# A two-layer bias-and-mix kernel: TensorE tiles of 64x64 and 64x32, and ten regions in place of nine

## What is computed

```python
# layer 0: x[h, q, k] += bias[q, k, h]
rel = tril(q - k)
nd = log(|c * rel| + 1) / (log(|c * max(rel.max(-1), threshold)| + 1) + 1e-6)
bias = relu(nd[..., None] * W1 + b1) @ W2 + b2
# layer 1, on x of shape (M=16, T=1024, S=1024)
ret = einsum('MTS,MN->NTS', x, w + eye)
ret += einsum('ITS,TIM->MTS', einsum('MTS,TIM->ITS', x, qw1), qw2)   # rank 2, per row t
ret += einsum('ITS,SIM->MTS', einsum('MTS,SIM->ITS', x, kw1), kw2)   # rank 2, per column s
ret += x * qdd[t, m] + x * kdd[s, m]                                 # diagonals
```

## Time and profile before

| | us |
|---|---|
| median of 3 runs | 911.21 |
| lowest and highest run | 910.2, 916.39 |
| span of the profiled execution | 930.2 |

### The profile page before, as it was taken

The page is one execution under the profiler, slowest core; times in us unless marked ns, Lnnn a source line. Parts: engine busy times, 40 slices in busy tenths (PEclk is TensorE's granted clock), DMA queues, the critical chain, the costliest instruction groups (busy, mean ns, idle before and its releaser), DMA issues. The chain is left out here.

```text
span 930.2 us, 39085 instructions
## 1 busy us (share of the span) xinstructions
PE 741.4 (80%) x18210; PEld 547.7 (59%) x18210; DVE 452.3 (49%) x483; ACT 387.6 (42%) x412; POOL 432.9 (47%) x267
## 2 busy tenths in 40 slices
PE   0678864798678876898799978999689878897984
PEld 0255654576556655666557745677357645676974
DVE  7496522376345533564346524464336524464352
ACT  3958624553463435543433334344233342341200
POOL 3545421254233432365458745586358753581020
PEclk9888887999999999999999999999899988999997
DMA  6787687658975999587976898488875988589068
GB/s 132 183 172 140 147 180 167 145 100 190 194 180 125 183 184 201 124 183 161 223 156 129 174 181 192 94 172 172 182 162 110 199 178 151 106 176 227 5 155 200
DMA packets 301055, 149.63 MB, mean 161 GB/s; under 512 B 30045, under 2 KB 296669, under 8 KB 300893
## 3 DMA queue, kind: packets, MB, share of 16 engines
q1 hardware_dynamic: 231456, 113.56, 56.9%
q10 hardware_dynamic: 69436, 33.58, 17.0%
HBM read 77.61 MB, written 69.47 MB: 158 GB/s over the span
## 5 line engine op out<-in xcount | busy, mean ns | idle before, releaser
L451 POOL TENSOR_TENSOR hidden<-log_table,row_scale 128x1024 f32<-128x1024 f32 x192 | 365.4, 1917 | 367.4 <-PE bias L757 359.5
L743 PE MATMUL main<-homes,mats_b 32*32 32x120 f32 (+1 forms) x9216 | 286.5, 272 | 119.6 <-issue 83.3
L743 PEld LDWEIGHTS main<-homes,mats_b 32*32 32x32 f32 x9216 | 257.9, 133 | 187.5 <-issue 136.1
L490 ACT ACTIVATE hidden<-hidden,b_col 128x1024 f32<-128x1024 f32 x192 | 220.3, 1149 | 310.3 <-POOL hidden L451 205.1
L732 PEld LDWEIGHTS main<-homes,mats_a 32*32 32x32 f32 x8192 | 238.1, 129 | 78.6 <-issue 54.9
L732 PE MATMUL main<-homes,mats_a 32*32 32x128 f32 x8192 | 258.8, 275 | 23.7 <-issue 23.6
L657 DVE SCALAR_TENSOR_TENSOR homes<-bias,b_col,homes 64x512 f32<-64x512 f32 (+1 forms) x256 | 185.8, 747 | 174.9 <-DMA homes<-in_x 106.5
L757 PE MATMUL bias<-hidden,w_blocks 128*64 128x512 f32 x768 | 207.6, 648 | 17.7 <-DVE b_col L620 8.8
L639 DVE TENSOR_TENSOR homes<-main,homes 128x1024 f32<-128x1024 f32 x128 | 156.8, 1225 | 107.7 <-PE main L732 104.6
L629 DVE COPY homes<-main 128x960 f32<-128x960 f32 x64 | 74.1, 1157 | 179.7 <-PE main L743 179.5
L517 ACT ACTIVATE homes<-main 128x960 f32<-128x960 f32 (+1 forms) x80 | 71.1, 891 | 109.4 <-PE main L743 99.3
(11 more groups left out here) (37 smaller groups left out, 32.2 us busy)
## 6 DMA issues: line engine op xcount, KB each, us to landing
homes<-in_x SPq DMA_DIRECT2D x200, 192.0 KB, 6.5
out_mixed<-homes ACTq DMA_DIRECT2D x104, 192.0 KB, 5.9
out_mixed<-homes SPq DMA_DIRECT2D x104, 192.0 KB, 5.6
homes<-in_x SPq DMA_DIRECT2D x72, 256.0 KB, 7.1
homes<-in_x SPq DMA_DIRECT2D x136, 64.0 KB
mats_in<-a_mats SPq DMA_DIRECT2D x128, 64.0 KB
out_mixed<-homes ACTq DMA_DIRECT2D x28, 256.0 KB, 8.0
out_mixed<-homes SPq DMA_DIRECT2D x28, 256.0 KB, 5.8
```

What stands on the lines that cost most here:

```text
L451: nc.gpsimd.tensor_tensor(hidden_tile(u, g).rearrange("p (j s) -> p j s", j=ROWS), bass.AP(logs.tensor, logs.offset, [list(logs.ap[0]), [1 ...
L490: nc.scalar.activation(hidden_tile(u, g), hidden_tile(u, g), ACT.Relu, bias=b1_col[:, 0:1])\
L743: mm = pe.matmul(main[of_group(g), i % 2, j * W:j * W + REGION_TILES[k] * ROWS], b_weights(g, C * ROWS + j), y_column(k, g, C * ROWS + j), ...
```

## The change

- `a_rows` addresses 64 partitions at once: two 64x64 tiles of the array with four blocks on the diagonal, in place of four 32x32. The weights need twice the columns, so a unit of `mats_a` is 8 rows (`UNIT = 8`) with the same 512 elements, written by two GpSimd operations of 128x256, and there are three units instead of two.
- `bias_tile` uses blocks of W2 of 64x32, each over 64 partitions (two slots) into one quadrant of 32 PSUM partitions, so eight matmuls per tile. Which quadrant a half feeds depends on the parity of the row (`(h + b) % 2`), and so the log table has a second copy for odd rows, shifted by two slots. In the first half the columns are cut into two parts of 256, and `add_bias` reads them with four operations in place of two.
- The regions become 8, eight times 14, and 8 tiles; the homes have 14 tiles. Pieces of loads and stores are cut to fit, `chunk_behind` asks for weight chunks at other tiles.
- Scratch tensors of the startup move within `homes`; `own_block` gets four columns in two steps.

The diff, cut to its core:

```diff
-REGION_TILES = (8,) + (15,) * 8
+REGION_TILES = (8,) + (14,) * 8 + (8,)
-STORE_PIECES = {8: (2, 3, 3), 15: (2, 3, 3, 3, 4)}
-LAST_STORES = (2, 3, 3, 3, 2, 1, 1)
-LOAD_PIECES = {8: (1, 3, 4), 15: (1, 3, 3, 3, 4, 1)}
+STORE_PIECES = {8: (2, 3, 3), 14: (2, 3, 3, 3, 3)}
+LAST_STORES = (2, 2, 2, 1, 1)
+LOAD_PIECES = {8: (1, 3, 4), 14: (1, 3, 3, 3, 3, 1)}
-UNIT = 16
-A_UNIT = H * GS * UNIT
+WIDE = 2
+RGP = WIDE * GP
+A_RING_UNITS = 3
+UNIT = 8
+A_UNIT = RGP * UNIT
...
-        log_table = sb("log_table", [P, TABLE])
+        log_table = sb("log_table", [P, 2, TABLE])
-        w2_blocks = sb("w2_blocks", [P, 2, P // 2])
+        w2_blocks = sb("w2_blocks", [P, GP])
...
         def place_of_unit(w):
-            return place_of_row((w - 1) * UNIT_TILES - 1) if w >= 2 else (0, COL_TILES - 4)
+            return place_of_row(w - A_RING_UNITS) if w >= A_RING_UNITS else (0, COL_TILES - 4)
         def chunk_behind(u):
-            if u == 0:
-                return A_RING
-            v, odd = divmod(u + 2 * CHUNK_TILES + 1, CHUNK_TILES)
-            return v if odd == 0 and A_RING < v < CHUNKS else None
+            v, odd = divmod(u + 2 * CHUNK_TILES - 2, CHUNK_TILES)
+            return v if odd == 0 and A_RING <= v < CHUNKS else None
...
             def spread_unit(w):
-                if w >= 2:
-                    pool.wait_ge(main_ready, a_tile_of((w - 1) * UNIT_TILES - 1) + 1)
...
-                nc.gpsimd.tensor_tensor(
-                    mats_a[:, w % 2 * A_UNIT:(w % 2 + 1) * A_UNIT].rearrange("p (n b e) -> p n b e", n=H, b=GS),
-                    rows.unsqueeze(2).to_broadcast([P, H, GS, UNIT]),
-                    bass.AP(own_block, 0, [[GS, P], [0, H], [1, GS], [0, UNIT]]), ALU.mult).then_inc(unit_ready, 1)
+                if w >= A_RING_UNITS:
+                    pool.wait_ge(main_ready, a_tile_of(w - A_RING_UNITS) + 1)
+                at = v % A_RING * H * CHUNK + part * UNIT
+                for q in range(WIDE):
+                    spread_half = nc.gpsimd.tensor_tensor(
+                        bass.AP(mats_a, w % A_RING_UNITS * A_UNIT + q * GP * UNIT,
+                                [[A_RING_UNITS * A_UNIT, P], [GS * UNIT, H], [UNIT, GS], [1, UNIT]]),
+                        bass.AP(mats_in, at, [[A_RING * H * CHUNK, P], [CHUNK, H], [0, GS], [1, UNIT]]),
+                        bass.AP(own_block, q * GS, [[WIDE * GS, P], [0, H], [1, GS], [0, UNIT]]), ALU.mult)
+                spread_half.then_inc(unit_ready, 1)
...
                     nc.gpsimd.tensor_tensor(
-                        hidden_tile(u, g).rearrange("p (j s) -> p j s", j=ROWS),
+                        hidden_tile(u, g).rearrange("p (j b s) -> p j b s", b=2, s=W),
+                        bass.AP(log_table, t0 - SLOTS * W * g, [[2 * TABLE, P], [2, ROWS // 2], [TABLE + 1, 2], [1, W]]),
+                        bass.AP(row_scale, t0 % PART, [[PART, P], [2, ROWS // 2], [1, 2], [0, W]]),
...
+            step(dve.tensor_scalar(log_table[:, 1, :], log_table[:, 0, :], slot_col[:, 1:2], 0.0, ALU.subtract, ALU.max))
...
             def add_bias(k, T):
                 for b in range(2):
-                    add = dve.scalar_tensor_tensor(
-                        out=y_rows(rows, k, T, b), in0=falling(u, b, 0 if both else b * (P // 2), P if both else P // 2),
-                        scalar=b2_col[rows, 0:1], in1=x_rows(rows, k, T, b), op0=ALU.add, op1=ALU.add)
+                    if groups_of(u) == 2:
+                        add = dve.scalar_tensor_tensor(
+                            out=y_rows(whole, k, T, b), in0=falling(u, b), scalar=b2_col[:, 0:1],
+                            in1=x_rows(whole, k, T, b), op0=ALU.add, op1=ALU.add)
+                        continue
+                    for part in range(2):
+                        some = slice(part * (ROWS // 4), (part + 1) * (ROWS // 4))
+                        add = dve.scalar_tensor_tensor(
+                            out=y_rows(low_half, k, T, b)[:, some], in0=falling_part(u, part, b),
+                            scalar=b2_col[low_half, 0:1], in1=x_rows(low_half, k, T, b)[:, some],
+                            op0=ALU.add, op1=ALU.add)
...
             def a_rows(k, T):
                 for n in range(ROWS):
-                    for g in range(GROUPS):
+                    for g in range(GROUPS // WIDE):
                         j = staggered(n, g)
-                        mm = pe.matmul(main[of_group(g), i % 2, j * W:(j + 1) * W], a_weights(g, w, part * ROWS + j),
+                        mm = pe.matmul(main[of_wide(g), i % 2, j * W:(j + 1) * W], a_weights(g, w, j),
                                        y_row(k, T, g, j), start=True, stop=True)
...
             def bias_tile(u):
                 for b in range(2):
                     for g in range(groups):
-                        into = low_half if (g if groups == 2 else b) == 0 else high_half
-                        rows = hidden_tile(u, g).rearrange("p (j b s) -> p b j s", s=W, b=2)[:, b]
-                        mm = pe.matmul(bias[into, u % 2, b * BANK:(b + 1) * BANK], w2_blocks[:, g, :], rows,
-                                       start=True, stop=True)
+                        for part in range(3 - groups):
+                            for h, of in enumerate((low_half, high_half)):
+                                q = 2 * (g + part) + (h + b) % 2
+                                n = ROWS // 2 // (3 - groups)
+                                rows = hidden_tile(u, g)[of, :].rearrange("p (j b s) -> p b j s", s=W, b=2)
+                                mm = pe.matmul(bias[quadrant(q), u % 2, b * BANK:b * BANK + n * W], w2_blocks[of, :],
+                                               rows[:, b, part * n:(part + 1) * n, :], start=True, stop=True)
```

More of the change, by code:

```diff
@@ L96, in build @@
         turned = term
-        first = {"a": spare_2[:, 6144:6400], "b": spare_2[:, 6400:6656]}
-        second = {"a": spare_2[:, 6656:6912], "b": spare_2[:, 6912:7168]}
+        first = {"a": spare_0[:, 3328:3584], "b": spare_0[:, 3584:3840]}
+        second = {"a": spare_0[:, 3840:4096], "b": spare_0[:, 4096:4352]}
         diag = {"a": spare_0[:, 2048:2176], "b": spare_0[:, 2176:2304]}
@@ L102, in build @@
         w2_rows = spare_0[:, 2688:2704]
+        own_halves = spare_0[:, 2704:2704 + GROUPS * GS]
         scale_late = spare_0[:, 2816:2816 + PART]
@@ L228, in x_landed, with quadrant @@
             return x_in[i], times(load_pieces, i, k) * PER_PIECE
+        def quadrant(q):
+            return slice(GP * q, GP * (q + 1))
         low_half, high_half, whole = slice(0, P // 2), slice(P // 2, P), slice(0, P)
@@ L374, in _ @@
             for k in range(REGIONS):
-                while k + 1 < REGIONS and loaded[k + 1] < 5:
+                while k + 1 < REGIONS and loaded[k + 1] < min(5, len(load_pieces(k + 1))):
                     load_x(k + 1, loaded[k + 1])
@@ L696, in _ @@
             pe.wait_ge(relu_b1_made, 1)
-            pe.matmul(bias[high_half, 1, 0:1], w2_blocks[:, 1, :], relu_b1[:, 0:1], start=True, stop=True)\
-              .then_inc(const_bias_made, 1)
+            for h, rows in enumerate((low_half, high_half)):
+                pe.matmul(bias[quadrant(GS + h), 1, 0:1], w2_blocks[rows, :], relu_b1[rows, 0:1], start=True, stop=True)\
+                  .then_inc(const_bias_made, 1)
             pe.wait_ge(const_bias_read, 1)
@@ L724, in a_rows @@
                 i = a_tile(k, T)
-                w, part = divmod(tile_of(k, T), UNIT_TILES)
+                w = tile_of(k, T)
                 pe.wait_ge(unit_ready, w + 1)
```

68 lines of the change are left out of this document (33 added, 35 removed).

## The result

Ten regions with the new tiles take 938.0 us (median of 4 runs, 931.8 to 941.0) against 910.7 (median of 4 runs, 903.5 to 916.4) of the kernel before: a ratio of 1.032, with an interval of 1.026 to 1.039. The kernel got slower by 3.2%; the forecast was 2.3% faster, 890 us with a range of 862 to 928. Some executions of one and the same kernel are a few per cent longer than the others: times here are medians of all executions, and ratios leave the long ones out, so that the two can differ in the third digit.

What follows compares the result with a forecast made beforehand. Column phases bound by transfers and code fetching, row phases by TensorE, the last region by idle transfers. 48 + 79 + 3 x 95.0 + 4 x 97.7 + 125 = 928, less 5 and 14: 909 us, scaled by 0.977 to 890; range 862 to 928.

Steps and rivals of the forecast that it cites:

- 125 us for the last 22 tiles: Region 8 (71 us: columns 40, rows 31) plus the last region (54), where 83.1 went for the last 15 tiles.
- 9.3 us of fetching: Full regions: these stalls stay per column phase, the rest shrinks with the tiles, giving 95.0 us three times, 97.7 four times.
- a third to a half of what the bias matmuls save: Column phases of regions 4 to 7: this share of 6.4 us let through, since transfers bind there.
- full regions above 97 us: Sign that the forecast is wrong; it expected full regions near 94 us.
- Rival 1: Full regions shrink further, to 90 us: 882 as profiled, 864 in the measure of the runs; chance 0.12.
- Rival 4: A region's length does not follow its tiles (chain of latencies): 972 as profiled, 952 in the runs; chance 0.08.
- Chunks of weights are asked for two row tiles later: Weight loads in SP's queue: its wait for GpSimd shrinks, but it waits for a store anyway; effect nothing.
- Rival 3: Bias matmuls run only four at a time, so their gain goes: 926 as profiled, 907 in the runs; chance 0.10.
- the 14 us of part 3: Regions 4 to 7: shorter row phases (37 us) and bias savings in column phases, together 3.5 us per region.
- 7 us for the extra bias instructions: Column phases: added code fetching, set against 12 us back in rows, net -5 us.
- Rival 5: 64-wide weight loads not hidden: 3.8 us per row tile, up to 243 us on top, above 1,000; chance 0.05.
- Rival 2: GpSimd binds row phases fully: 935, so 916 (chance 0.13); with dear spreads about 966, so 946 (0.07).

Runs made afterwards that it cites:

- e5: The kernel before, unchanged, profiled a second time: span 916.1 us, 917.9 as timed, beside runs with a median of 913.5.
- e1: The kernel before with only the regions changed to ten (8, eight times 14, 8): 952.8 us, ratio 1.038 to the kernel before.
- e7: e1 with half of the column matmuls left out, so the output is incomplete: 857.8 us (one execution).
- e2: The changed kernel with three weight chunks in turn instead of two, each asked for five row tiles earlier: 931.9 us, ratio 1.016 to the kernel before.
- e4: e1 plus the 64x32 bias matmuls; rows, units and chunk loads as before: 951.1 us, ratio 1.038 to the kernel before.
- e12: e2 without its bias part (bias matmuls, log table and additions as before): 940.6 us, ratio 1.035 to the kernel before.
- e10: e1 with each bias matmul of 512 columns cut into two of 256: 956.6 us, ratio 1.052 to the kernel before.
- e3: e1 plus 64x64 row matmuls, their units and late chunk loads; bias as before: 931.0, 944.5, 959.4 and 1056.4 us, no ratio.

## Why the prediction was wrong, point by point

The forecast was a sum of 909 us for the profiled execution, and the profile has 934.5; then it was scaled by 911.2/930.2, where the changed kernel's median, 938.0, lies above its span. In figures each of the two is about half of the 48 us between 890 and 938. As causes they are not equal.

**The scale.** The profiled execution of before was taken as one that stands in a fixed ratio to the median. It does not: e5 spans 916.1 us, and its timed value is 1.8 above its span. Some 14 us of the 930.2 belonged to that execution. But its slowness was also in the rows from which the terms were taken, and scaling took out again what had gone in so. The same rules on the rows of e5 give 48 + 79.5 + 662.6 + 125 - 19 = 896 against 916.1, again a ratio of 0.978. It was the terms that failed:

| change in us | forecast, from the 930.2 | measured, from e5 |
|---|---|---|
| seven full regions | -62.3 | -36.0 |
| what comes after them | +41.9 | +56.1 |
| startup and region 0 | -0.8 | -1.7 |
| all | -21.2 | +18.4 |

**The ten regions: the term that failed.** One step was "Hence 125 us for the last 22 tiles". With the regions alone (e1) these tiles took 93.0 + 59.1 = 152.1 us, in the changed kernel 81.8 + 57.6 = 139.4. Region 8 was given 40 us of columns because little was left to load; it took 49.3. TensorE was busy for 36.6 of it, at a clock of 0.90, where 30.5 had been summed, and idle for 12.7 in place of 9.3. The last region was given 54 and took 57.6.

The other step was that the column phase of a full region shrinks with its tiles but for 9.3 us of fetching, and then by a third to a half of what the bias matmuls save. The row phases came out as forecast (42.4 us in e5, 38.2 in e1, 37.0 after). The column phases gave nothing: 58.4, 57.8 and 58.6. It is luck that the forecast's 3 x 95.0 + 4 x 97.7 = 676 us before any relief lies near e1's 671.9: it came from the slower trace, and the same rule on e5 gives 662.6.

From nine to ten regions e5 to e1 loses 705.3 - 671.9 = 33.4 us for seven tiles taken out of the full regions and pays 152.1 - 83.3 = 68.8 us for putting them at the end. The difference of the two, 35.4, less 2.2 us by which e1 gets to region 1 earlier (125.3 against 127.5), is the difference of the spans, 33.2. A column phase of 16 steps with 1,024 matmul instructions is what each region must have, also the one of 8 tiles: 30.7 us in e1, with DMA at 29%. The forecast counted a fixed part of 9.3 us per region; the runs with 15, 14 and 12 tiles show some 21, all of it in columns. What fills a column phase when its tiles get fewer is open: e7 shows a part for TensorE and one for x, not why the sum stays. The forecast's own sign, full regions above 97 us, did not show (95.6), but it was set against the 930.2; against e5 the limit is (916.1 - 48 - 79.5 - 125)/7 = 94.8. Rival 1, full regions of 90, is refuted. Rival 4, the length that does not follow the tiles, was true in part, for some 21 us of 100 rather than all of it.

**GpSimd's queue: the step that was waved through.** "Chunks of weights are asked for two row tiles later relative to their spread, so SP's wait for GpSimd shrinks ... nothing." It is three tiles later, not two. SP's wait did shrink (68.1 us in e5, 10.5 after), but I did not ask who waits at the other end. It was GpSimd, 95.2 us, with the hidden tiles queued behind the spread. e2 prices it at 1.6% by the ratios, some 15 us, and at 5.5 us by the two traces. The reason given for "nothing" was right as far as it went: SP's wait moved to the next store (106.3 us in all before, 194.3 after, first line below), and the chunk loads stand behind that store.

SP's own waits in the changed kernel (us in total, times, the longest):

```profile
SPq L273 <- DVE homes L647: 194.3, 21, 27.2
SPq L330 <- POOL mats_a L435: 10.5, 7, 3.0
```

**Bias matmuls.** Their price was right: 1.09 us for the record of 16 instructions where 1.07 was forecast, and 0.66 for 0.63 (the next row tile begins 1.02 and 0.60 us after their start). Rival 3 is refuted, and with it the literal reading of the rule that the forecast quoted from the Trainium skill ("TensorEngine Tiling (Array Packing)", Restrictions and Gotchas), that different row tiles cannot use one PSUM bank at the same time. But the 14 us of part 3 that they and the rows were to bring to the full regions did not arrive: these take 669.3 us against e1's 671.9. Of that, 5.5 us are the late chunks (e2 has 663.8). For the rest the runs point to fetching. The sum gave it 7 us for the extra bias instructions; in e4's trace it is 88 us. Between e12 and e2 it is 45 us (61 to 106), while TensorE's busy time falls by 65, and the difference of 20 us is about the gain of 1.9% (the two traces differ by 8.6 us). The part of this that remains open: e10 with nearly as many instructions as e4 waits 128 us, not 181. It may be that instructions in short bursts call for code faster than the same number spread out; that was only argued. That e4's trace is of its longest execution would fit too.

**Row matmuls.** 64 instructions, two tiles, take 4.20 us, where 128 took 3.86 (127 of them 3.79 in the earlier trace rows):

```profile
822.60 3.86 PE L732 MATMUL main<-homes,mats_a 32*32 32x128 f32 x128
```

Two tiles are thus slower by 0.34 us, 22 us over the kernel if all of it lay on the path; forecast was no change. So one takes 2.10, where the forecast named 2.1 as the bound of being right. The rule quoted from the Trainium skill ("TensorE: Matmul & The Clock Gate", Part 3, Packing small matmuls), that a weight load overlaps matmuls in flight only when its row group differs, does not set the time here: loads of 64 columns are recorded at 204 ns against 129, and a pass takes (4.20 - 0.28)/32 = 122 ns (0.28 is the record of the last matmul) where the streaming alone was put at 107. Rival 5 is refuted. Waits before row matmuls fell from 23.6 us to 0.2, better than half.

**GpSimd's prices.** 615 ns for a spread (601 forecast), 37.7 us for a row phase of the second half (37 forecast), GpSimd busy for 37.5 of it. VectorE's addition of 256 took 480 ns (500 forecast). Rival 2 is refuted.

**The clock** (theory 3) was in no term. The full regions ran at a mean of 0.95 in e5, 0.93 in e1 and 0.90 after. Half speed is one of two levels (1.2 and 2.4 GHz), so 0.90 is a fifth of the time at 1.2 GHz. In the changed kernel the column phases of regions 1 to 8, in which TensorE waits, had 0.78 to 0.90, the row phases 1.00 but for one with 0.95. By the overlap of matmuls with stretches at 1.2 GHz they lie there for 90 us in e5, 116 in e1 and 128 after, of which half is lost: 45, 58 and 64. So some 13 to 19 us of the slowdown could pass through the clock. No run holds the clock apart from the rest, so this is a size and not a cause shown; and in e12, with a ratio near e1's, the matmuls have only 98 us at 1.2 GHz.

Taken together, in ratios: ten regions +3.8% (e1), wide rows and small bias tiles with early chunks -2.2% (e1 to e2), late chunks +1.6% (e2 to the changed kernel), which makes the measured 3.2%; the last step compares two chips. No kernel among these beats the one before.

## What to carry to other kernels

Price a further stage or region by what it must do whatever its size (here 16 column steps and 1,024 matmul instructions), and read that from runs with different sizes before moving work to a short last stage. Look at the phases of a stage one by one: here a stage with fewer tiles got shorter in rows and not in columns. When a request is moved later in one queue, look at who stands first in line for it and what is queued behind him. A matmul form that saves array time with more instructions is worth only as much as code fetching leaves of it; count both. And take the rows from two executions where they can be had: a full region of the same kernel had 102.8 us in one and 100.8 in the other.

## What the runs showed of the hardware

- Eight 64x32 tiles of the array work at once in float32: 16 matmul instructions of 512 columns take 1.09 us, where four at a time would take 1.9 (rival 3). Two row groups write the same PSUM bank meanwhile, on different partitions.
- A float32 pass of 128 columns takes 112 ns (3.86/32 less its tail) on four 32x32 tiles and 122 on two 64x64; its weight load is hidden in both.
- Code comes to TensorE in pieces of 16 KB. Waits for it were 0.39 to 1.1 us per piece, by kernel (47 us for 119 pieces in e3, 181 for 161 in e4), and were longest in the kernel with bias tiles as bursts of 16 and rows of 64 instructions (e4). Nothing here shows why. Nearly all of them (48 of 49 in the changed kernel) end 1.2 to 1.8 us after such a piece has landed.
- A GpSimd multiplication of 128x256 with runs of 8 elements costs 615 ns: the short runs add 14 ns, 2%, to what 1.71 ns per element and 163 ns would make it.
